# Idle TensorE matmuls rearranged in the opening of a graph-network layer: one, three and nine instead of three, none and three

## The chip, the cores and the metric

One core of a Trainium2 chip runs the whole kernel. The metric is the device time of one execution in microseconds (us). Below, PE is TensorE (its weight loads are PEld), DVE is VectorE, ACT is ScalarE, POOL is GpSimd and SP is the sync engine, which issues the transfers.

## The reference

There are 12500 nodes of width 128 and 200000 edges of width 48, sorted by the node that receives them.

```
h = relu(layernorm(x))
agg = segment_sum(edge_attr, dst, 12500)
z1 = silu(concat(h, agg) @ W1 + b1)        # 176 -> 256
z2 = silu(z1 @ W2 + b2)                    # 256 -> 256
out = x + h + z2 @ W3 + b3                 # 256 -> 128
```

## The kernel before

The nodes are cut into 28 tiles of 448, the edges into groups of 512 (4 edges for each of 128 partitions) and 28 batches of 14 groups and a short last one. A group reaches at most 42 neighbouring nodes, its window. Its segment sum is four small matmuls: the raw edges (128x48) against a one-hot matrix (128x42) that DVE makes by comparing the index rows with a ramp (`make_onehot`, L786). `sum_tile` (L1109, L1112) issues these for a batch: the first seven groups go straight to their place in a bank, the other seven to a staging bank that ACT copies out (`stage_sums`, L554) and POOL adds into `agg_carry` (L498).

The opening prepares the indices, and most of what the change touches lies there. In order of the dependences:

- POOL makes `ident`; PE clears the banks with three matmuls (L1040, L1041) and then runs `WARM0` idle matmuls (L1043). An idle matmul multiplies `ident` by `ident` into a bank nobody reads then. It appears in the trace as two records, as every fp32 matmul does.
- DVE computes the first 128 groups' relative indices (`rel_rows`, L731) and goes on with small index arithmetic until L753. PE turns those rows (`turn_rows(0)`, L1033, four transposes), ACT copies them to `rel` (`rel_of(0)`, L546), and DVE makes the first one-hot matrices (L786).
- ACT makes the other relative rows (L540); `turn_rows(1)`, `turn_rows(2)` and `turn_rows(3)` turn them. The second waits for the offsets that DVE copies (L814), the third follows the loading of offset registers.
- PE then issues `sum_tile(0)`, waits for `s_small` and `s_rel`, counts invalid groups (L1212, L1214), runs `WARM2` idle matmuls (L1217), and issues `sum_tile(1)`, whose last wait is for the one-hot matrices of batch 1. Between them, DVE works a serial list: one-hot matrices of batch 0, the statistics of the first x tile (L761 to L771), two reductions (L725), small steps up to L833, one-hot matrices of batch 1 with `shift_of_norm` (L779) between.
- After `sum_tile(1)` come the turning of the normalized nodes (L1123), the first layer, and the pipeline over the tiles. DVE's `carry_over(0)` (L917) waits for batch 1's sums and for POOL's seven additions of batch 0.

ACT zeroes part of `agg_carry` in two pieces (`clear_carry`, L535): one ahead of `rel_of(0)`, one behind `rel_of(3)` and ahead of the W1 splits (L568, L571). SP issues the transfers of the opening from a fixed list.

Of the kernel before, what the change touches and what calls it, by code (L numbers as in the profile page):

```python
# [33 lines left out]
def gnn_kernel(nc, x, dst, edge_attr, W1, b1, W2, b2, W3, b3, out):  # L34
# [3 lines left out]
    P = 128  # L38
# [10 lines left out]
    TILE = NPG * GPT  # L49
# [11 lines left out]
    ROWS = 4  # L61
# [15 lines left out]
    LOOP, PE_LOOP = (4, 20, 4), (2, 26, 2)  # L77
    LATE_ZEROS = LOOP[0] - 1
    XSLOTS = 4
    WARM0, WARM2 = 3, 3  # L80
    DUMP = 2 * BANK
    NODES = NT * TILE + OVER
    STEPS = NT + 3
# [20 lines left out]
    with ExitStack() as ctx:  # L104
        def sb(name, shape, dt=F32):
            return ctx.enter_context(nc.sbuf_tensor(name, shape, dt))

        def ps(name, shape, dt=F32):
            return ctx.enter_context(nc.psum_tensor(name, shape, dt))

        def sem(name):
            return ctx.enter_context(nc.semaphore(name))
# [14 lines left out]
        ident = sb("ident", [P, P])  # L127
# [26 lines left out]
        agg_carry = sb("agg_carry", [ED, NODES + WINDOW])  # L154

        POOL_ZEROS = 2 * TILE
        ACT_ZEROS = (POOL_ZEROS, 15 * TILE, 20 * TILE)
        POOL_LATE = [(t * TILE, (t + 1) * TILE) for t in range(20, 24)]
        ZEROED = POOL_LATE[-1][1]
        COPIED = NT * TILE - ZEROED  # L160
# [44 lines left out]
        tp = ps("tp", [P, BANK])  # L205
# [35 lines left out]
        s_rel = sem("rel_ready")  # L241
# [63 lines left out]
        def where_invalid(eng, engine_type, body):  # L305

            eng.wait_ge(s_invalid, 1)
            _, (flag,) = nc.values_load_multi_w_load_instructions(
                any_invalid[0:1, 0:1], engines=[engine_type], min_val=0, max_val=NG,
                skip_runtime_bounds_check_because="it counts groups")  # L310
            with eng.If(flag):
                body()
# [140 lines left out]
        def _(pool):  # L453
# [28 lines left out]
            def nodes_of(b):  # L482
                _, nodes = nc.values_load_multi_w_load_instructions(
                    staged_row[0:1, bass.ds(b * SLOT, HALF)], engines=[mybir.EngineType.Pool],
                    min_val=0, max_val=NODES,
                    skip_runtime_bounds_check_because="a valid group's first node is a node, else it is the centre")
                return nodes
# [37 lines left out]
        def _(act):  # L525
# [8 lines left out]
            def clear_carry(a, b):  # L534
                act.activation(agg_carry[:, a:b], zeros[0:ED, :].broadcast_to([ED, b - a]),  # L535
                               ACT.Copy).then_inc(s_carry0_act, 1)
# [6 lines left out]
            def rel_of(c):  # L543
                n = P if c < FULL_ROWS else LAST_G
                act.wait_ge(s_relT, c + 1)
                act.activation(rel[:, c * P:c * P + n, :], rows_turned(c).rearrange("p j r -> p r j"),  # L546
                               ACT.Copy).then_inc(s_rel, 1)
# [9 lines left out]

            clear_carry(*ACT_ZEROS[0:2])
            rel_of(0)
# [3 lines left out]
            for c in range(1, ROWS):  # L563
                rel_of(c)
            clear_carry(*ACT_ZEROS[1:3])
            act.wait_ge(s_w1, W1_LOADS)
# [455 lines left out]
        def _(pe):  # L1022
# [19 lines left out]
            for _ in range(WARM0):  # L1042
# [4 lines left out]
                      start=True, stop=True).then_inc(s_small0T, 1)  # L1047
# [25 lines left out]
            def batch_of(b):  # L1073

                if not isinstance(b, int):
                    return 0, GPT
                return (SHIFT if b == 0 else 0), min(GPT, NG + SHIFT - b * GPT)

            def offsets_of(b):
                first, last = batch_of(b)  # L1080
                _, offsets = nc.values_load_multi_w_load_instructions(
                    direct_row[0:1, bass.ds(b * SLOT, min(last, HALF) - first)], engines=[mybir.EngineType.PE],
                    min_val=0, max_val=DUMP,
                    skip_runtime_bounds_check_because="valid groups lie within SLACK of their tile")
                return offsets
# [3 lines left out]
            def sum_tile(b, parity, offsets):  # L1089

                first, last = batch_of(b)
                wait(pe, s_staged, b)
                wait(pe, s_clear, min(b - 1, NT - 2) if isinstance(b, int) else b - 1)
                for half in range(2):
                    if half * HALF < last:
                        _, _, n, full = groups_of(b, half)
                        slot = 2 * parity + half
                        pe.wait_ge(s_edges[slot], 16 * slot_turn(b, parity) + (16 if full < n else 0))
                        pe.wait_ge(s_onehot, 2 * b + half + 1)
                for at in range(HALF):  # L1100
                    for j in range(PER):
                        for half in range(2):
                            if not first <= at + half * HALF < last:
                                continue
                            rows = P if at < groups_of(b, half)[3] else TAIL_P
                            edges = raw[0:rows, 2 * parity + half, at, j, :]
                            into = onehot[0:rows, 2 * parity + half, at * PER + j, :]
                            if half == 0:
                                mm = pe.matmul(banks[0:ED, bass.ds(offsets[at - first], WINDOW)], edges, into,  # L1109
                                               start=False, stop=True, skip_group_check=True, tile_position=(0, 0))  # L1110
                            else:
                                mm = pe.matmul(stage[ROW2:ROW2 + ED, at * WINDOW:(at + 1) * WINDOW], edges, into,  # L1112
                                               start=(at == 0 and j == 0), stop=True, skip_group_check=True,
                                               tile_position=(0, ROW2))
                mm.then_inc(s_summed, 1)
# [90 lines left out]
            turn_rows(3)  # L1206
            sum_tile(0, 0, offsets)
            offsets = offsets_of(1)
            pe.wait_ge(s_small, 2)
            pe.wait_ge(s_rel, ROWS)  # L1210
            for c in range(FULL_ROWS):
                pe.matmul(invalid_sum[:, 0:1], g["invalid"][:, c:c + 1], one[:, :],  # L1212
                          start=(c == 0), stop=(c == FULL_ROWS - 1))
            pe.matmul(invalid_sum[:, 1:2], g["invalid"][0:LAST_G, FULL_ROWS:ROWS], one[0:LAST_G, :],  # L1214
                      start=True, stop=True, skip_group_check=True).then_inc(s_invalidT, 1)
# [5 lines left out]
            for c in range(1, ROWS):  # L1221
                mm = pe.matmul(nodes_ps[0:PLACE_ROW + 1, c * P:(c + 1) * P], node_place[:, c, :], ident[:, :],
                               start=True, stop=True)
# [25 lines left out]
```

## Time and profile before

| what | value |
|---|---|
| median of 3 runs | 288.13 us |
| the three runs | 288.31, 288.13, 286.89 us |
| profiled execution, its own time | 288.73 us |
| its span | 287.0 us |
| mean granted TensorE clock over the span | 0.994 |

The profile is of one execution. Its span runs from the first to the last instruction, and 1.73 us lie around it. The granted clock is a share of TensorE's full speed: 1.00 is 2.4 GHz, 0.50 is 1.2 GHz. The page shows 1.00 where no change of the clock has been recorded yet, so for the start the durations of the matmuls have to be read as well.

### The profile page before, as it was taken

To read this page: it belongs to the slowest core of one execution; us is meant where nothing else is said; L and a number is where in the kernel's file an instruction comes from. 1 tells how busy PE (TensorE), PEld (TensorE's weight loads), DVE (VectorE), ACT (ScalarE), POOL (GpSimd) and SP (SyncE) were. 2 spreads that over 40 slices of the span, in tenths; PEclk is the share of its full clock that TensorE was granted. 3 is DMA by queue.
4 is the path that set the end of the run, shared out by engine and by line. 5 is a ranking of instruction groups with operands and counts; after the bars stand their busy time and mean duration, and the time that the engine had idled before them with its cause. 6 is when DMAs were issued, how large, how long until landed. Compare 5 with 4: busy or idle time off the path is not lost.

```text
span 287.0 us, 11959 instructions
## 1 busy us (share of the span) xinstructions
PE 274.2 (96%) x4286; PEld 248.4 (87%) x4287; DVE 241.2 (84%) x583; ACT 220.3 (77%) x424; POOL 135.7 (47%) x248
## 2 busy tenths in 40 slices
PE   7868999999999999999999999999999999999994
PEld 3756988999999999999999999999999999999793
DVE  7887998889898898998998889989898888986551
ACT  8856778787886888778877788787976878779662
POOL 4275565454455445454555446454455445452200
PEclk9979999999999999999999999999999999999999
DMA  6998965865688457865687547955687567820112
GB/s 168 323 306 249 204 171 147 248 187 166 170 251 246 142 158 221 256 178 162 182 246 218 173 137 240 256 168 162 187 251 224 149 170 227 253 82 21 30 38 62
DMA packets 79309, 53.28 MB, mean 186 GB/s; under 512 B 2984, under 2 KB 78850, under 8 KB 79288
## 3 DMA queue, kind: packets, MB, share of 16 engines
q1 hardware_dynamic: 79288, 53.04, 63.6%
q8 instruction: 8, 0.13, 0.2%
q14 instruction: 13, 0.11, 0.1%
HBM read 46.29 MB, written 6.40 MB: 184 GB/s over the span
## 4 chain that ended last, share of the span: by engine, by line
PE 85%; DVE 5%; issue 3%; ACT 3%; POOL 2%; ACTq 0%; POOLq 0%; DVEq 0%
PE agg_ps L1109 21%; PE z L1176 15%; PE z L1157 7%; PE z L1161 7%; PE z L1158 7%; PE agg_ps L1112 4%; PE z L1137 4%; PE tp L1123 4%; PE z L1143 4%; PE z L1142 3%; PE z L1139 3%; PE z L1138 3%; DVE onehot L786 2%; PE agg_ps L1040 1%; POOL agg_carry L498 1%
## 5 line engine op out<-in xcount | busy, mean ns | idle before, releaser
L498 POOL TENSOR_TENSOR agg_carry<-staged,agg_carry 48x42 f32 x196 | 92.8, 474 | 77.1 <-ACT staged L554 46.3
L1109 PEld LDWEIGHTS agg_ps<-onehot,raw 128*48 128x48 f32 x1560 | 73.6, 126 | 12.1 <-issue 12.1
L1109 PE MATMUL agg_ps<-onehot,raw 128*48 128x42 f32 x1560 | 77.0, 216 | 3.5 <-DVE onehot L786 3.5
L786 DVE TENSOR_TENSOR onehot<-window,rel 128x1176 f32<-128x1176 f32 (+1 forms) x57 | 77.5, 1363 | 0.5 <-ACT rel L546 0.5
L1112 PE MATMUL agg_ps<-onehot,raw 128*48 128x42 f32 x1568 | 77.2, 216 | 0.0
L1112 PEld LDWEIGHTS agg_ps<-onehot,raw 128*48 128x48 f32 x1568 | 73.9, 127 | 0.0
L479 POOL TENSOR_TENSOR rstd<-vareps,minus_half 128x4 f32<-128x4 f32 (+1 forms) x28 | 37.7, 1346 | 46.4 <-DVE vareps L771 46.4
L1176 PE MATMUL z<-w,h 128*128 128x128 f32 x392 | 51.2, 282 | 1.5 <-ACT h L625 1.1
L625 ACT ACTIVATE h<-z,b2c 128x448 f32<-128x448 f32 (+1 forms) x56 | 35.4, 633 | 19.5 <-PE z L1161 17.1
L1176 PEld LDWEIGHTS z<-w,h 128*128 128x128 f32 x392 | 46.0, 191 | 3.2 <-ACT z L621 1.4
L941 DVE TENSOR_TENSOR h_lo<-h,h_hi 128x448 fp32r<-128x448 f32 (+1 forms) x56 | 34.8, 624 | 12.1 <-ACT h_hi L639 7.6
L635 ACT ACTIVATE h<-z,b1c 128x448 f32<-128x448 f32 (+1 forms) x56 | 35.0, 624 | 11.5 <-PE z L1143 11.5
L1157 PE MATMUL z<-h_hi,w_hi 128*128 128x448 f32 (+1 forms) x112 | 43.1, 385 | 0.0
L593 ACT ACTIVATE xn<-x_t,nmr,rstd 128x128 f32<-128x128 f32 x98 | 40.2, 478 | 1.3 <-DVE nmr L779 1.3
L1158 PE MATMUL z<-h_hi,w_lo 128*128 128x448 f32 (+1 forms) x112 | 40.7, 363 | 0.0
L639 ACT ACTIVATE h_hi<-h 128x448 fp32r<-128x448 f32 (+1 forms) x56 | 32.3, 576 | 1.8
L917 DVE TENSOR_TENSOR agg<-agg_ps,agg_carry 48x448 f32<-48x448 f32 (+1 forms) x28 | 17.2, 614 | 17.5 <-PE agg_ps L1112 17.3
L1161 PE MATMUL z<-h_lo,w_hi 128*128 128x448 f32 (+1 forms) x112 | 31.6, 363 | 0.0
L607 ACT ACTIVATE agg_hilo<-agg 48x448 fp32r<-48x448 f32 (+1 forms) x28 | 16.1, 575 | 11.7 <-DVE agg L917 11.7
L1161 PEld LDWEIGHTS z<-h_lo,w_hi 128*128 128x128 f32 x112 | 21.0, 188 | 1.6
L1158 PEld LDWEIGHTS z<-h_hi,w_lo 128*128 128x128 f32 x112 | 21.1, 189 | 1.2
L1157 PEld LDWEIGHTS z<-h_hi,w_hi 128*128 128x128 f32 x112 | 21.1, 188 | 1.2
(129 smaller groups left out, 411.9 us busy)
## 6 DMA issues: line engine op xcount, KB each, us to landing
raw<-in_edge_attr_dram SPq DMA_DIRECT2D x55, 672.0 KB, 5.9
x_t<-in_x_dram SPq DMA_DIRECT2D x14, 256.0 KB, 6.1
out_dram<-out_t SPq DMA_DIRECT2D x13, 256.0 KB
out_dram<-out_t SPq DMA_DIRECT2D x14, 192.0 KB, 6.0
x_t<-in_x_dram SPq DMA_DIRECT2D x13, 192.0 KB, 6.2
dst_rows<-in_dst_dram SPq DMA_DIRECT2D x1, 512.0 KB
agg_carry<-agg_carry SPq DMA_DIRECT2D x1, 336.0 KB, 8.0
raw<-in_edge_attr_dram SPq DMA_DIRECT2D x1, 288.0 KB, 3.6
```

The source lines that it names most:

```text
L479: pool.tensor_tensor(rstd[:, parity, 0:n], vareps[:, 0:n], minus_half[:, 0:n], ALU.pow).then_inc(s_rstd, 1)
L498: pool.tensor_tensor(into, staged[:, parity, n, :], into, ALU.add).then_inc(s_added, 1)
L593: ln = act.activation(xn[:, parity, q, :], x_t[:, turn, q, :], ACT.Identity, bias=nmr[:, parity, q:q + 1], scale=rstd[:, parity, q:q + 1])
L625: act.activation(h2[:, m, parity * TILE:parity * TILE + n], z[:, m, 0:n], ACT.Silu, bias=b2c[:, m:m + 1]).then_inc(s_h2, 1)
L635: act.activation(h1[:, m, 0:n], z[:, m, 0:n], ACT.Silu, bias=b1c[:, m:m + 1]).then_inc(s_h1, 1)
L786: return dve.tensor_tensor(onehot[:, slot, at * PER:n * PER, :], window[:, :].unsqueeze(1).broadcast_to([P, cols_n, WINDOW]), cols.unsquee ...
L1109: mm = pe.matmul(banks[0:ED, bass.ds(offsets[at - first], WINDOW)], edges, into, start=False, stop=True, skip_group_check=True, tile_posit ...
L1112: mm = pe.matmul(stage[ROW2:ROW2 + ED, at * WINDOW:(at + 1) * WINDOW], edges, into, start=(at == 0 and j == 0), stop=True, skip_group_chec ...
L1157: pe.matmul(z[:, m, 0:n], w2_hi[:, k, cols], h1_hi[:, k, 0:n], start=(k == 0), stop=False)
L1158: pe.matmul(z[:, m, 0:n], w2_lo[:, k, cols], h1_hi[:, k, 0:n], start=False, stop=False)
L1161: mm = pe.matmul(z[:, m, 0:n], w2_hi[:, k, cols], h1_lo[:, k, 0:n], start=False, stop=(k == M - 1))
L1176: mm = pe.matmul(into[0:np_], h2[:, k, a:a + np_], w3[:, k, :], start=False, stop=(k == M - 1), skip_group_check=True)
```

## The change

The idle matmuls in front of the first turns go from three to one (`WARM0`). Three new ones (`WARM1`) are issued behind `sum_tile(0)` and its register loads; the wait for `s_rel` is put in front of them, since they write the bank `tp` that `rel_of(3)` reads. The idle matmuls in front of `sum_tile(1)` go from three to nine (`WARM2`). The border between ACT's two pieces of zeros moves from column 15 x 448 to column 14 x 448, so that 448 columns go from the first piece to the second.

```diff
-    WARM0, WARM2 = 3, 3
+    WARM0, WARM1, WARM2 = 1, 3, 9
...
-        ACT_ZEROS = (POOL_ZEROS, 15 * TILE, 20 * TILE)
+        ACT_ZEROS = (POOL_ZEROS, 14 * TILE, 20 * TILE)
...
             sum_tile(0, 0, offsets)
             offsets = offsets_of(1)
+            pe.wait_ge(s_rel, ROWS)
+            for _ in range(WARM1):
+                pe.matmul(tp[:, 0:P], ident[:, :], ident[:, :], start=True, stop=True)
             pe.wait_ge(s_small, 2)
-            pe.wait_ge(s_rel, ROWS)
             for c in range(FULL_ROWS):
```

## Rows read from the trace of the kernel before

**Rows 1.** The page: busy time of PE, its 40 slices, the granted clock.

```profile
PE 274.2 (96%) x4286; PEld 248.4 (87%) x4287; DVE 241.2 (84%) x583; ACT 220.3 (77%) x424; POOL 135.7 (47%) x248
...
PE   7868999999999999999999999999999999999994
...
PEclk9979999999999999999999999999999999999999
```

**Rows 2.** Windows of 20 us: length, busy of PE, PEld, DVE, ACT, POOL, granted clock, DMA, GB/s.

```profile
0.00:20.00 20.00, 14.02 (x160) 9.90 (x163) 17.52 (x69) 15.67 (x20) 9.32 (x31) 0.95 0.93 261
...
60.00:80.00 20.00, 20.00 (x315) 18.50 (x314) 17.95 (x40) 15.99 (x32) 9.56 (x17) 1.00 0.68 197
```

**Rows 3.** The chain that ended last, in order of time: start, us, what.

```profile
6.11 1.58 PE tp L1043 x6
7.69 0.55 PE z L1033 x4
...
8.27 0.60 ACT rel L546
...
8.90 0.68 DVE onehot L786
...
17.04 1.31 DVE onehot L786
```

**Rows 4.** Windows by stage, columns as in rows 2; the last two of tile agg_ps alone.

```profile
14.50:18.50 4.00, 1.31 (x15) 1.01 (x14) 3.90 (x12) 2.66 (x8) 2.98 (x4) 0.94 1.13 296
18.60:21.30 2.70, 2.70 (x68) 2.70 (x70) 1.63 (x9) 0.70 (x2) 2.00 (x6) 0.50 1.08 317
...
18.50:22.60 4.10, 3.95 (x112) 3.83 (x112) 0.04 (x1) 0.04 (x1) 0.65 1.01 291
28.30:31.10 2.80, 2.72 (x112) 2.61 (x112) 0.00 (x1) 0.00 (x0) 1.00 1.10 183
```

**Rows 5.** Matmuls by line: records, ns min/median/max, first and last start.

```profile
L1043 PE MATMUL tp<-ident x6: 421/421/582, 6.0 to 7.3; 128*128 128x128 f32 x6
...
L1033 PE MATMUL z<-ident,rel_rows x12: 273/285/412, 7.5 to 10.7; 128*128 128x128 f32 x12
...
L1217 PE MATMUL tp<-ident x6: 275/275/377, 16.0 to 16.7; 128*128 128x128 f32 x6
```

**Rows 6.** Timeline of PE: start, us, operation, records, idle before and its releaser.

```profile
11.82 1.50 PE L1112 MATMUL agg_ps<-onehot,raw 128*48 128x42 f32 x29
...
15.66 0.29 PE L1212 MATMUL z<-one,g_invalid 128*1 128x1 f32 x6 [1.12 <-DVE node_place L833]
...
15.99 0.94 PE L1217 MATMUL tp<-ident 128*128 128x128 f32 x6
18.57 0.30 PE L1109 MATMUL agg_ps<-onehot,raw 128*48 128x42 f32 x1 [1.64 <-DVE onehot L786]
```

**Rows 7.** Timeline of DVE in the opening.

```profile
5.83 0.49 DVE L731 TENSOR_SCALAR rel_rows<-dst_rows,g_middle 128x512 f32<-128x512 int32 x1
...
8.18 0.20 DVE L753 TENSOR_SCALAR node_place<-g_moved,g_valid 128x1 f32<-128x1 f32 x1
...
15.44 0.16 DVE L833 TENSOR_SCALAR node_place<-g_chosen 128x3 f32<-128x3 f32 x1
```

**Rows 8.** Timeline of ACT in the opening.

```profile
2.27 5.04 ACT L535 ACTIVATE agg_carry<-zeros 48x5824 f32<-48x5824 f32 x1
...
12.02 2.06 ACT L535 ACTIVATE agg_carry<-zeros 48x2240 f32<-48x2240 f32 x1
14.25 0.42 ACT L568 ACTIVATE w1x_hi<-out_t 128x256 fp32r<-128x256 f32 x1 [0.17 <-DMA out_t<-in_L_gnn_W_dram]
```

**Rows 9.** Timeline of POOL: the last addition of batch 0.

```profile
20.33 0.25 POOL L498 TENSOR_TENSOR agg_carry<-staged,agg_carry 48x42 f32 x1 [0.17 <-POOL agg_carry L498]
```

**Rows 10.** The second load of edges of batch 0: issue, and us to landing.

```profile
L348 SPq DMA_DIRECT2D raw<-in_edge_attr_dram x1: 389/389/389, 5.1 to 5.1; - x1
...
DMA to landing us min/median/max: 5.9/5.9/5.9
```

## The prediction

> **What bounds the kernel now.** I read the page first: PE is busy for 96% of the span, and its slices stand at 9 from the fifth on [rows 1]. The windows sharpen this: PE is busy for all of 20 us in the steady stretch, but for 14.02 us of the first 20 [rows 2]. So the steady part can only be shifted: whatever makes PE start it earlier moves the end by as much, unless another engine or a transfer holds it back. The slices of the granted clock have one dent, in the third [rows 1]. The chain of waits then says what sets the time in the opening, and the windows by stage say at which clock. The reader is to see two places in them.
>
> The first is the way to the first one-hot matrix. It runs through the three idle matmuls, the first turns, ACT's copy and then DVE at 8.90 [rows 3]. The relative rows were there at 5.83 + 0.49 = 6.32 [rows 7], while the turns could be issued only behind the idle matmuls. These ran at half the clock: a record of L1043 took 421 ns, one of the same shape in L1217 took 275 ns [rows 5].
>
> The second is the sum of batch 1. PE waits 1.64 us for DVE's one-hot matrix and starts at 18.57 [rows 6]; the chain comes there from DVE [rows 3]. Before it PE did 1.31 us of work in 4.00 us, and the granted clock fell within that stretch; from 18.60 to 21.30 it stood at 0.50, that is 1.2 GHz, and PE was busy throughout [rows 4].
>
> **The change part by part.** *Two idle matmuls fewer in front of the first turns.* Six records of L1043 take from 6.11 to 7.69, 1.58 us with what overlaps [rows 3]; their starts from 6.0 to 7.3 give about 0.21 us a record once they flow [rows 5]. Four records are thus 0.85 us, and the turns could start 0.85 us earlier, at about 6.63 instead of 7.48, which is still behind the relative rows at 6.32. Four turns were partly at full clock and will now all be at half: 3 x 0.21 + 0.41 = 1.04 us, so they end at 7.67 instead of 8.24: 0.57 us earlier. ACT is free then, as its first clear ended at 2.27 + 5.04 = 7.31 [rows 8] and gets shorter. Its copy of 0.60 us ends at about 8.30. DVE, however, is busy until 8.18 + 0.20 = 8.38 [rows 7], and starts the one-hot matrix at about 8.40 instead of 8.90: a head start of 0.50 us.
>
> Does it reach 18.57? From there DVE works its list with few holes. I looked for waits of its list on others: the x tile, the offsets, POOL's rstd. None of these shows as DVE's releaser except the short one ahead of the first one-hot, so the whole list should move by 0.50. PE's first sums move with it, from 11.82 to 11.32 [rows 6]; the edges they need land at 5.1 + 5.9 = 11.0 [rows 10], which leaves 0.3 us of cover and no more. Beyond that cover the sums would be late, but not DVE's list, which is what counts. Transfers issued behind the sums don't move, because SP is still busy with its fixed list then. I take 0.50 us; the bounds are 0 (something on DVE's list holds it) and 0.57.
>
> *Three idle matmuls behind the first sums.* In the trace PE idles there for 1.12 us until DVE's node_place [rows 6]. Three cost at most 0.94 us, the busy time of the six records of L1217 [rows 6]. The new place of the wait for `s_rel` costs nothing: ACT's last copy ended before its second clear began at 12.02 [rows 8], and the invalid count behind it waits for the same node_place. Cost 0; without the cover, 0.94 us on a count that DVE needs only at the end of its one-hot matrices.
>
> *Nine instead of three in front of the second sums.* With the head start, the count goes from 15.66 to 15.16 and the idle matmuls start at 15.49. Nine cost at most 3 x 0.94 = 2.82 us; without the 0.275 us tail of each set they flow at (0.94 - 0.275)/5 = 0.13 us a record, 18 x 0.13 = 2.4 us. They end between 17.9 and 18.3. The sums can start at 18.57 - 0.50 = 18.07. So they lie in PE's wait, or run over it by at most 0.24 us. I take 0, by the flowing record, since a following matmul doesn't wait for the tail.
>
> *What they do to the clock.* PE's work between 14.5 and 18.5 goes from 1.31 us to roughly 1.3 + 0.8 + 1.6 = 3.7 us of 4. In the trace no stretch so filled lost the clock: it stood at 1.00 wherever PE was busy for nearly all of a window [rows 2, 4]. So I expect the fall to stay away. Its price is read from two batches of the same 112 records: 3.95 us for batch 1, against 2.72 us for batch 2 at full clock [rows 4]. That is 1.23 us. The bounds are 0 (it falls in spite of this) and 1.23.
>
> *Zeros.* A column costs 5.04/5824 = 0.87 ns, so 448 are 0.39 us [rows 8]. The first clear ends at 6.92, in ACT's wait. The second starts 0.5 us earlier, at 11.5, and ends at 11.5 + 2.06 + 0.39 = 13.97, ahead of the W1 transfer that released ACT at 14.25 [rows 8]. Cost 0. If the head start fails, it ends at 14.47 and delays the staged sums by 0.2 us; POOL's additions then end at 20.58 + 0.2, still ahead of the need below.
>
> *Who is late next.* Batch 1's sums end at 18.07 + 2.72 = 20.8 instead of 22.5. DVE's carry_over also needs POOL's last addition of batch 0, 20.33 + 0.25 = 20.58 [rows 9]: 0.2 us of cover, and a bound of 0.2 us on the gain if DVE's work slows POOL more.
>
> **The sum.** -0.50 - 1.23 = -1.73 us, from 288.73 to 287.00 for the profiled execution. That execution was 0.60 us above the median, 288.13, so the median comes to 286.4 us.
>
> **The rivals.**
> *The clock term is missing in the comparison.* One of the three runs took 286.89 us, 1.2 to 1.4 us less than the others, which is the size of the clock's price. Perhaps that execution had no fall. If the typical execution has none, or the fall comes in spite of the idle matmuls, only 0.50 us stay: 287.6 us. For it: the three times spread by just that size. Against it: two of three, and the profiled one, are the long kind. The Trainium skill (TensorE: Matmul & The Clock Gate, Part 1) says that the clock is judged in steps not tied to the start of the kernel, so the same kernel differs from run to run; the one trace here can't show that.
>
> *The head start is lost.* DVE's list is held by a wait that now has slack, or the nine idle matmuls run over: 286.9 us. For it: 0.24 and 0.2 us of cover.
>
> *Everything is given back.* A stretch behind 23 us is set by transfers, and PE waits longer there: 288.1 us. Against it: PE's later waits name DVE and ACT, and DMA was at 0.68 in the steady stretch [rows 2].
>
> *Slower: the clock rises later.* Here it reached full speed during the first turns [rows 5]. With 0.85 us less of idle matmuls ahead, it may stay at half through the first sums. These end at 11.3 + 2 x 2.72 = 16.7. Behind them at half clock come three idle matmuls, 6 x 0.21 = 1.3 us, the count, about 0.6, and nine, 18 x 0.21 = 3.8, so the second sums start at 22.4, and end at 25.1 even at full clock instead of 22.5: +2.6 us, 290.7 us. It decides once the second sums end later than 22.5 + 1.4, so only if half clock lasts through most of the first sums. Against it: the idle matmuls and turns flow almost unbroken from 2 us on, and PE's clock stood at 1.00 over the stretch of turns behind.
>
> A rule speaks for this rival. The turns of 9.5 to 11 us ran at 0.285 us a record, like the fast idle ones [rows 5]; so a stretch made mostly of turns kept the full clock. The Trainium skill (TensorE: Matmul & The Clock Gate, Part 4) says that transposes don't count as PE work for the full clock. By that rule the removed matmuls count and the turns in their place don't, and the time would be this rival's 290.7 us; by the trace, which disagrees as far as keeping the clock goes, it is 286.4 us.
>
> **How the numbers follow.** 0.5% of 288.13 is 1.44 us, about what can be told from no change; faster means below 286.69. Chances: forecast 0.53, clock term missing 0.17, head start lost 0.13, everything given back 0.09, clock rises later 0.08. The forecast's own range is 285.9 to 286.9, and some of it (0.08 of the 0.53) is above 286.69; faster gets 0.45 of it and 0.02 of the lost head start, 0.47. Slower is the last rival, 0.08, and the rest, 0.45, is same. The range leaves out the last rival and the edges: 285.8 to 288.1.
>
> **What would show it.** Right: first turns at about 6.6, first one-hot at 8.4; 24 idle records between the two sums (six and eighteen, where there were six); granted clock 1.00 from 14 to 23; the second sums from 18.1 to 20.8, and the same shift at 28.34 and in the first layer. Wrong: first one-hot still at 8.9; the clock at 0.50 anywhere behind 8 us; PE's wait on DVE gone in front of the second sums because the idle matmuls end later; DVE's carry_over released by POOL; or the shift lost between 23 and 40 us. The forecast fails most easily if other executions have the clock's changes elsewhere than this one.

## The result and the profile after

| | before | after |
|---|---|---|
| median, 12 executions each | 288.22 us | 289.67 us |
| ratio after to before | | 1.0062, interval 1.0040 to 1.0084 |
| profiled execution, its own time | 288.73 us | 290.63 us |
| its span | 287.0 us | 288.9 us |
| its mean granted clock | 0.994 | 0.987 |

The change makes the kernel slower by 0.6%: 1.8 us by the ratio, 1.45 us by the medians. 286.4 us was forecast, in a range of 285.8 to 288.1. The sign is that of the rival to which I gave 0.08. All ratios leave out executions more than 1.5% above the fastest of their kernel; there is one such, in e11 below.

The page of the changed kernel, busy time of PE and granted clock in 40 slices, beside [rows 1]:

```profile
PE 277.3 (96%) x4300; PEld 250.8 (87%) x4301; DVE 241.3 (84%) x583; ACT 220.6 (76%) x424; POOL 133.8 (46%) x248
...
PEclk9779999999999999999999999999999999999999
```

The dent has become two slices wide and starts one slice (7.2 us) earlier. PE's timeline of the changed kernel shows what fell into it; compare [rows 6]:

```profile
6.63 1.06 PE L1033 MATMUL z<-ident,rel_rows 128*128 128x128 f32 x4
...
10.48 1.65 PE L1033 MATMUL z<-ident,rel_rows 128*128 128x128 f32 x8 [1.64 <-ACT rel_rows L540]
...
17.49 1.30 PE L1211 MATMUL tp<-ident 128*128 128x128 f32 x6
18.73 0.29 PE L1214 MATMUL z<-one,g_invalid 128*1 128x1 f32 x6
...
19.06 2.27 PE L1219 MATMUL tp<-ident 128*128 128x128 f32 x18
...
21.27 0.24 PE L1109 MATMUL agg_ps<-onehot,raw 128*48 128x42 f32 x1
```

Its DVE and ACT, beside [rows 3]: the first and the last one-hot matrix ahead of the second sums, then ACT's second set of relative rows and the last of its copies (`rel_of(3)`).

```profile
8.36 0.68 DVE L786 TENSOR_TENSOR onehot<-window,rel 128x504 f32<-128x504 f32 x1
...
16.34 1.38 DVE L786 TENSOR_TENSOR onehot<-window,rel 128x1176 f32<-128x1176 f32 x1
```

```profile
9.71 1.95 ACT L540 ACTIVATE rel_rows<-dst_rows,g_minus_middle 128x512 f32<-128x512 int32 x3 [1.39 <-DMA dst_rows<-in_dst_dram]
...
12.89 0.19 ACT L546 ACTIVATE rel<-tp 128x28 f32<-128x28 f32 x1
```

The windows by stage, beside [rows 4]; columns as there:

```profile
8.85:10.45 1.60, 0.00 (x0) 0.00 (x0) 1.55 (x6) 0.74 (x2) 0.00 (x0) 1.00 1.00 332
10.48:12.10 1.62, 1.62 (x8) 1.13 (x8) 1.59 (x9) 1.62 (x3) 0.07 (x1) 0.81 1.11 344
11.60:18.00 6.40, 6.29 (x89) 5.77 (x88) 5.95 (x17) 5.24 (x10) 2.74 (x5) 0.50 1.04 288
12.90:16.90 4.00, 4.00 (x75) 4.00 (x76) 3.90 (x11) 3.65 (x5) 1.87 (x4) 0.50 1.09 297
21.34:23.99 2.65, 2.65 (x112) 2.53 (x112) 0.00 (x0) 0.00 (x0) 0.83 (x1) 1.00 1.12 328
```

And the chain that ended last, 8 to 24 us, its longest pieces:

```profile
4.81 4.88 DMA dst_rows<-in_dst_dram
10.48 1.65 PE z L1033 x8
12.85 2.48 PE agg_ps L1112 x29
17.49 1.30 PE tp L1211 x6
19.13 2.21 PE tp L1219 x18
```

The reader is to see that the chain no longer comes to the second sums from DVE. It starts at the transfer of the index rows, which landed at 9.71 and released ACT, and then runs through PE alone but for ACT's first piece. DVE was ready at 16.34 + 1.38 = 17.72, 0.6 us earlier than before, as forecast. PE had nothing to do between 8.85 and 10.45. The mean of 0.81 over the 1.62 us that follow means half clock for 0.38 x 1.62 = 0.6 us of them, so the clock fell about 1 us behind the idle stretch, and the first sums ran at 1.2 GHz. They ended at 17.49, against some 14.5 before: 1.0 us of this is the later start behind the index rows, 1.9 us the half clock (4.64 us for the sums instead of 2.7). Only then came the trio, the count and the nine, and the chain goes through both groups of idle matmuls. The second sums started at 21.27, 3.55 us after DVE was ready. They ran at full clock and ended at 23.99, where those of before ended at 22.5. This 1.5 us is close to the difference of the medians. The profiled execution, 1.0 us above its kernel's median, lost about 0.5 us more between 42 and 53 us, which I did not follow: PE's node turns (L1123) of before start at 40.89 and 51.02, those of the changed kernel at 42.36 and 52.97.

### The profile page after: what moved, and what is told of

Same layout as the page of the kernel before. It is cut to its first block, busy times and chain, and to the rows that moved or that the text cites. A ratio compares the mean times of both kernels' runs of the same rounds, so it can differ in the third digit from the quotient of the medians.

```text
span 288.9 us, 11986 instructions
## 1 busy us (share of the span) xinstructions
PE 277.3 (96%) x4300; PEld 250.8 (87%) x4301; DVE 241.3 (84%) x583; ACT 220.6 (76%) x424; POOL 133.8 (46%) x248
## 4 chain that ended last, share of the span: by engine, by line
PE 85%; ACT 3%; issue 3%; DVE 2%; DMA 2%; SPq 1%; POOL 1%; ACTq 0%; POOLq 0%; DVEq 0%
PE agg_ps L1109 21%; PE z L1176 15%; PE z L1157 7%; PE z L1158 7%; PE z L1161 7%; PE agg_ps L1112 5%; PE z L1137 4%; PE tp L1123 4%; PE z L1143 3%; PE z L1142 3%; PE z L1139 3%; PE z L1138 3%; DMA dst_rows<-in_dst_dram 2%; POOL agg_carry L498 1%; DVE onehot L786 1%
## 5 line engine op out<-in xcount | busy, mean ns | idle before, releaser
L498 POOL TENSOR_TENSOR agg_carry<-staged,agg_carry 48x42 f32 x196 | 91.0, 464 | 81.3 <-ACT staged L554 52.6
L635 ACT ACTIVATE h<-z,b1c 128x448 f32<-128x448 f32 (+1 forms) x56 | 35.0, 624 | 11.5 <-PE z L1143 11.5
```

The lines of the kernel that those rows point to most:

```text
L498: pool.tensor_tensor(into, staged[:, parity, n, :], into, ALU.add).then_inc(s_added, 1)
L635: act.activation(h1[:, m, 0:n], z[:, m, 0:n], ACT.Silu, bias=b1c[:, m:m + 1]).then_inc(s_h1, 1)
```

## The experiments

All times are medians of 10 to 12 executions; the ratio is to the kernel before on the same chip, and is not the quotient of the two medians beside it, from which it differs by up to 0.3%. The three numbers name the idle matmuls at the front, behind the first sums, and ahead of the second sums; "gap" are those that I put between L1046 and the second turns. The kernel before is 3, 0, 3 and the changed one 1, 3, 9.

| run | idle matmuls | us | before, us | ratio, interval |
|---|---|---|---|---|
| e1 | 1, 0, 3 | 287.04 | 287.35 | 0.9981, 0.9965 to 0.9998 |
| e2 | 3, 3, 9 | 289.96 | 287.35 | 1.0063, 1.0036 to 1.0089 |
| e3 | 1, 3, 3 | 288.29 | 287.35 | 1.0025, 1.0009 to 1.0042 |
| e4 | 3, 0, 3, zeros moved | 287.50 | 287.35 | 0.9997, 0.9973 to 1.0020 |
| e5 | 3, 0, 9 | 288.67 | 287.58 | 1.0016, 0.9995 to 1.0037 |
| e6 | 1, gap 4, 3, 9 | 287.87 | 287.58 | 1.0003, 0.9986 to 1.0021 |
| e7 | 1, gap 4, 0, 3 | 287.55 | 287.58 | 1.0002, 0.9981 to 1.0022 |
| e8 | 1, 0, 0 | 287.00 | 287.58 | 0.9970, 0.9952 to 0.9988 |
| e9 | 1, gap 4, 0, 8 | 287.59 | 287.55 | 0.9993, 0.9971 to 1.0014 |
| e10 | 1, 0, 9 | 288.82 | 287.55 | 1.0047, 1.0028 to 1.0067 |
| e11 | 0, 0, 0 | 286.80 | 287.55 | 0.9971, 0.9949 to 0.9992 |
| e12 | 3, gap 4, 0, 3 | 287.68 | 287.55 | 1.0002, 0.9977 to 1.0026 |

Zeros are moved in e2, e3 and e6 too, as in the changed kernel. The results also give the mean granted clock of every execution, and it falls into steps: 1.00, 0.994, 0.988, 0.982. 0.988 means twice as much time at half clock behind the first recorded change as 0.994. In each of the six profiles that read 0.987 or 0.988 (after, e1, e2, e4, e8, e10) this is one unbroken stretch, twice as long as that of [rows 4]: from 11.5 to 18.3 us in the changed kernel, from 8.7 to 15.5 us in e1. In the profiles at 0.994 it is a short one, and it can lie early (e3, 11.3 to 14.6 us) or late (before, e7 and e12, from about 18 us). So the mean clock says how long the clock was down, not where. The count in each step, with the median of those executions:

| kernel | 1.00 | 0.994 | 0.988 | 0.982 |
|---|---|---|---|---|
| before, with e1 to e4 | 9: 287.21 | 16: 287.46 | 8: 287.81 | |
| before, with e5 to e8 | 7: 287.15 | 16: 287.51 | 12: 287.81 | |
| before, with e9 to e12 | 7: 286.84 | 13: 287.55 | 15: 287.63 | |
| after | | | 10: 289.60 | 2: 290.88 |
| e1 (1, 0, 3) | | | 12: 287.03 | |
| e2 (3, 3, 9) | 2: 287.37 | 1: 289.92 | 7: 290.05 | |
| e3 (1, 3, 3) | | 1: 287.50 | 9: 288.18 | 2: 289.05 |
| e4 (3, 0, 3, zeros moved) | 3: 287.08 | 6: 287.94 | 3: 287.57 | |
| e5 (3, 0, 9) | 2: 286.91 | 3: 288.08 | 7: 288.84 | |
| e6 (1, gap 4, 3, 9) | 9: 287.73 | 3: 288.52 | | |
| e7 (1, gap 4, 0, 3) | 4: 287.44 | 8: 288.03 | | |
| e8 (1, 0, 0) | | | 11: 286.99 | 1: 287.00 |
| e9 (1, gap 4, 0, 8) | 6: 287.56 | 6: 287.65 | | |
| e10 (1, 0, 9) | | 1: 288.05 | 9: 288.75 | 2: 289.38 |
| e11 (0, 0, 0) | 2: 287.84 | | 8: 286.55 | 2: 289.06 |
| e12 (3, gap 4, 0, 3) | 7: 287.18 | 4: 288.72 | 1: 289.56 | |

**Which part costs.** The first four runs each take one part alone or back.

```diff
-    WARM0, WARM2 = 3, 3
+    WARM0, WARM2 = 1, 3
```

> The kernel before with one idle matmul instead of three in front of the first turns; nothing else is changed. Theory 1: the fewer idle matmuls at the front decide about the clock, since PE then works less ahead of the first sums; the granted clock falls near 12 us and the first sums run at half clock, as in the profile of the changed kernel, where they ended at 17.49 instead of 14.54. The span's mean clock is then near 0.988 or below. Behind them come only three idle matmuls and no trio, so the second sums start near 19 us and the time is 287.5 to 288.5 us, less than the changed kernel's 289.7. Rival (the queue): the idle matmuls in front of the sums cost the time and the front does nothing; clock 0.994 as before, time 287.7 to 288.2 us.

The mean clock did as theory 1 said, 0.988 in all twelve. The time was 287.04 us, a little under before and below the forecast 287.5. So half clock in the first sums costs almost nothing by itself. In its profile the clock fell earlier than theory 1 had it, at about 8.7 us, and was back at 15.5. The window from 9 to 15 us, and PE ahead of the second sums:

```profile
9.00:15.00 6.00, 5.17 (x51) 4.82 (x53) 5.82 (x23) 5.69 (x9) 2.74 (x5) 0.50 1.10 320
```

```profile
16.99 0.29 PE L1212 MATMUL z<-one,g_invalid 128*1 128x1 f32 x6 [0.58 <-issue]
...
17.33 0.94 PE L1217 MATMUL tp<-ident 128*128 128x128 f32 x6
...
18.19 0.24 PE L1109 MATMUL agg_ps<-onehot,raw 128*48 128x42 f32 x1
```

The second sums start at 18.19, earlier than the 18.57 of [rows 6], although most of the first ran at half clock: PE's waits of 1.12 and 1.64 us had held room for that.

```diff
-    WARM0, WARM1, WARM2 = 1, 3, 9
+    WARM0, WARM1, WARM2 = 3, 3, 9
```

> The changed kernel with three idle matmuls at the front again: three, three and nine, zeros as changed. Theory 1: with the front back the clock stays up from the first turns through the second sums; mean clock 0.999 or so, second sums from about 18.6 to 21.3 us, 286.9 to 287.1 us. Rival (the queue): twelve idle matmuls between the sums push the second sums back; the time stays near 289.7 us.

Theory 1 falls here. Three at the front again, and the time stays at 289.96 us. The two executions in which the clock stayed up took 287.37, the seven at 0.988 took 290.05.

```diff
-    WARM0, WARM1, WARM2 = 1, 3, 9
+    WARM0, WARM1, WARM2 = 1, 3, 3
```

> The changed kernel with three instead of nine idle matmuls in front of the second sums: one, three and three. Its twelve records fewer at the 0.12 us that they took in the profile of the changed kernel (2.21 us for eighteen) are 1.5 us. Theory 1 with the queue as its price: the first sums still run at half clock, and the second sums start 1.5 us earlier, 288.2 us, if the clock has risen by then. If it has not, the second sums run at half clock and the time is 289.5 us or more. If the idle matmuls were all hidden, it stays at 289.7 us.

288.29 us, 1.4 us below the changed kernel's median (1.1 us by the ratios, 1.0025 against 1.0062): the six idle matmuls lay on the path. Against e1 the trio costs 1.25 us, together with the moved zeros, which the next run has alone.

```diff
-        ACT_ZEROS = (POOL_ZEROS, 15 * TILE, 20 * TILE)
+        ACT_ZEROS = (POOL_ZEROS, 14 * TILE, 20 * TILE)
```

> The kernel before with only the border of ScalarE's two pieces of zeros moved by 448 columns. Theory 1: no difference within 0.2 us, clock 0.994 as before. Rival (zeros): the longer second piece delays the weight splits and the staged sums, and the time rises by 0.2 to 0.4 us.

No difference that can be told: the interval, 0.9973 to 1.0020, is 0.8 us below to 0.6 us above, so the rival's 0.2 to 0.4 us is not excluded. Its profile also fell into an execution in which the kernel otherwise like before has the early fall:

```profile
12.90:16.90 4.00, 3.89 (x73) 3.76 (x72) 3.90 (x10) 3.02 (x5) 2.58 (x5) 0.50 1.10 291
```

```profile
16.91 0.29 PE L1212 MATMUL z<-one,g_invalid 128*1 128x1 f32 x6
...
17.24 1.46 PE L1217 MATMUL tp<-ident 128*128 128x128 f32 x6
18.67 0.23 PE L1109 MATMUL agg_ps<-onehot,raw 128*48 128x42 f32 x1
```

So the first sums at half clock are no product of the change alone. The profile I predicted from showed one kind of execution of before; this is another, in which PE comes to the count at 16.91 instead of 15.66 and there is no wait left for more idle matmuls to hide in.

**The queue theory and the gap theory.** My new theory had two parts. In executions whose first sums run at half clock, PE is late, and each idle matmul behind them delays the second sums (the queue). And the early fall comes from PE's idle stretch between L1046 and the second turns (the gap).

```diff
-    WARM0, WARM2 = 3, 3
+    WARM0, WARM2 = 3, 9
```

> The kernel before with nine instead of three idle matmuls in front of the second sums; front three, no trio. Queue theory: PE is late in the executions whose first sums run at half clock, so the six extra ones delay the second sums by 12 records x 0.12 = 1.4 us there, and lie in PE's wait for DVE in the executions at full clock. A third to two thirds of the executions of before are of the late kind, so the median is 287.6 to 288.8 us, with a spread between executions at 1.00 (near 287.2 us, as before) and the others. Clock theory (the one the prediction rested on): the nine keep the clock up for the second sums, 286.9 us or less.

As the queue theory says: 286.91 us in the two executions at full clock, 288.84 in the seven at 0.988, and 288.08 in the three between. The interval of the ratio still takes in 1, with executions that differ so.

```diff
+    MID = 4
...
                       start=True, stop=True).then_inc(s_small0T, 1)
+            for _ in range(MID):
+                pe.matmul(tp[:, 0:P], ident[:, :], ident[:, :], start=True, stop=True)
```

> The changed kernel with four more idle matmuls, placed in PE's wait between the turning of the first offsets and the second turns, where it idled 1.64 us in the changed kernel's profile; the other numbers stay one, three and nine. Gap theory: that idle stretch is what makes the clock fall near 12 us; filled, the clock stays at 1.00, the first sums end by 15 us, all twelve idle matmuls behind them are hidden again, and the time is 286.7 to 287.3 us, 2.5 us less than the changed kernel. Rival (the front decides, or the clock falls whatever is in the gap): the fall stays, mean clock 0.988, and the time is 289.7 us or up to 0.5 more.

This is the changed kernel with four idle matmuls more, and it is 1.8 us faster by the medians (ratio to before 1.0003 against 1.0062). Not one of its executions is at 0.988. PE in its profile, where the line numbers are three higher behind the new lines, and the window of the first sums:

```profile
8.77 1.16 PE L1050 MATMUL tp<-ident 128*128 128x128 f32 x8
9.88 1.30 PE L1034 MATMUL z<-ident,rel_rows 128*128 128x128 f32 x7
...
15.34 0.91 PE L1214 MATMUL tp<-ident 128*128 128x128 f32 x6 [0.46 <-issue]
...
16.51 2.28 PE L1222 MATMUL tp<-ident 128*128 128x128 f32 x18
...
18.71 0.24 PE L1112 MATMUL agg_ps<-onehot,raw 128*48 128x42 f32 x1
```

```profile
12.90:16.90 4.00, 3.54 (x86) 3.27 (x84) 3.90 (x11) 3.77 (x7) 2.15 (x4) 1.00 1.14 294
```

The time is 0.6 us above the 287.3 of the expectation. The nine end near 18.7, and the second sums start there, 1.1 us behind DVE, whose last one-hot matrix is ready at 17.65 in this profile. So even at full clock the twelve were not wholly hidden.

> One idle matmul at the front, four in the gap ahead of the second turns, none behind the first sums and three ahead of the second. Gap theory: mean clock 0.994 to 1.000; the 0.5 us of head start stays; 286.4 to 286.9 us, against 287.0 for the same kernel without the four. Rival (half clock in the first sums is hidden in PE's later waits anyway): no difference from 287.0 us. Rival (front decides): clock 0.988 and 287.0 us or more.

287.55 us: no gain over e1, as the second theory's rival had it. None of its executions is at 0.988, eight are at 0.994. The profiled one, 288.95 us, has the late fall of [rows 4]: the second sums start at 18.06, with 1.23 us of wait for DVE ahead, and run at half clock from about 18.3 to 21.7. The eight are not all alike: four took 287.3 to 287.6 us, as those at 1.00 did, and four 288.5 to 288.95, so only the latter look like the profiled one.

> One idle matmul at the front and none between the sums. Queue theory: where the first sums run at half clock, the three in front of the second sums are on PE's path too; without them the second sums start up to 0.9 us earlier, as soon as DVE's one-hot matrix is there (18.0 us): 286.2 to 286.7 us, against 287.0 with the three. Rival (the three hold the clock up for the second sums): these run at half clock more often, and the time is 287.5 to 288.3 us.

287.00 us, ratio 0.9970. None of the three is needed to bring the second sums to full clock in its profile:

```profile
16.85 0.29 PE L1212 MATMUL z<-one,g_invalid 128*1 128x1 f32 x6 [0.50 <-issue]
...
17.90 0.23 PE L1109 MATMUL agg_ps<-onehot,raw 128*48 128x42 f32 x1 [0.64 <-DVE onehot L786]
```

```profile
12.10:16.10 4.00, 4.00 (x79) 4.00 (x79) 3.90 (x10) 3.20 (x6) 2.61 (x5) 0.54 1.13 302
18.00:20.60 2.60, 2.60 (x112) 2.50 (x112) 1.58 (x9) 1.00 (x3) 1.76 (x7) 1.00 0.97 270
```

The first sums, stretched by the half clock, fill most of the time up to DVE, and the clock came back while they ran, at about 15.8 us, with no idle matmul ahead but the one at the front. The gain over e1 was to be 0.3 to 0.8 us: by the ratios it is 0.3 us, at the lower end and within both intervals.

**Doses and the ends.** Four more, cut from the same lines.

> One idle matmul at the front, four in the gap ahead of the second turns, none behind the first sums, eight ahead of the second. In the profile with three there, PE waited 1.23 us behind them, room for five more at 0.24 us each. Gap and queue theories together: the first sums and the second run at full clock in nearly all executions (mean clock 1.00), nothing runs over, 286.5 to 287.0 us. Rival (half clock in the first sums is hidden anyway, and DVE's list sets the start of the second): no better than one at the front and none between the sums, 287.0 us. If they run over DVE: 287.3 us or more.

The clock is better kept (six at 1.00, six at 0.994) and the second sums start at 18.06 and run at full clock in the profile, yet 287.59 us is no better than before. It did not do what I expected.

> One idle matmul at the front, no trio, nine ahead of the second sums: the changed kernel without the trio, with the old zeros. Queue theory: between one-and-three (287.0 us) and the changed kernel (289.7 us); six more than the first are 12 records x 0.12 = 1.5 us, of which up to 0.2 us may be hidden, so 288.3 to 288.6 us, and all executions alike, mean clock 0.988. Rival (the trio alone makes the loss): 287.0 to 287.3 us.

288.82 us; 1.8 us over e1 by the medians, 1.9 us by the ratios (0.0066 x 287.5). The six extra are on the path. With intervals of some 0.5 us either way on each ratio, this is no clear difference from the 1.5 us of their records.

> The kernel before with no idle matmul at all. If idle matmuls are worth something here, the second sums or the stretch behind run at half clock, and the time is 288.3 us or more (1.2 us for the second sums). If the first sums at half clock bring the clock up by themselves and the wait for DVE hides them, it is 286.7 to 287.3 us, like one at the front and none between the sums.

286.80 us, ratio 0.9971. None of the sets of idle matmuls tried here does better than none. Two things in its executions: the profiled one shows what the mean clock hides, as the page gives 1.00 where no rise has been recorded:

```profile
12.10:16.10 4.00, 4.00 (x78) 4.00 (x76) 3.86 (x12) 3.13 (x5) 2.71 (x5) 1.00 1.13 303
```

```profile
11.84 2.55 PE L1112 MATMUL agg_ps<-onehot,raw 128*48 128x42 f32 x29
...
18.00 0.30 PE L1109 MATMUL agg_ps<-onehot,raw 128*48 128x42 f32 x1 [0.93 <-DVE onehot L786]
```

29 records in 2.55 us instead of the 1.50 of [rows 6]: this was half clock, and a record of 0.30 us at 18.00, where e8 has 0.23, says that it still was when the second sums started. That execution took 287.86 us. And one of the twelve took 291.35 us.

> The kernel before with four more idle matmuls in the gap ahead of the second turns; three, none and three otherwise. Gap theory: the early fall near 12 us disappears, so mean clocks are 1.00 or 0.994 and none 0.988; where a fall remains it is the late one, ahead of the second sums, as in the first profile, and costs 1.2 us there: two kinds of executions, near 287.2 and near 288.5 us. Rival (the gap has nothing to do with it): the same mixture of clocks as the kernel before.

One of twelve at 0.988, where the gap theory had none, against 35 of the 103 executions of before; the rest in two kinds, 287.18 and 288.72 us, as the gap theory has it. The 1.5 us between them is near the 1.23 us that I took for second sums at half clock.

## Why the prediction was wrong, point by point

**The head start was right.** DVE's first one-hot matrix came at 8.36 (8.40 forecast, 8.90 before) and the last was ready at 17.72, 0.6 us earlier. e1, which has this part alone, is 0.3 us faster by the medians and 0.5 us by the ratio, which has an interval of 0.06 to 1.0 us.

**The zeros and the new place of the wait**: no cost shows. e4 has none beyond its interval. The wait was not tried alone, but in the changed kernel's profile ACT's last copy ended at 12.89 + 0.19 = 13.08, long before PE came to the wait at 17.49.

**The step that failed is the cover of the idle matmuls**, in the words of the prediction: "So they lie in PE's wait, or run over it by at most 0.24 us. I take 0", and for the trio "Cost 0; without the cover, 0.94 us". The waits of 1.12 and 1.64 us behind the first sums were read from one execution in which these ran at full clock. In the changed kernel's profile they took 4.64 us (12.85 to 17.49) instead of 2.7, and had started 1.0 us later, behind index rows that landed later. The late landing is not the change's doing: with the same front and zeros, e3's profile has its first sums at 11.52. The second sums waited for PE. In terms of that profile: PE came out of the first sums 2.95 us late; the trio, the count and the nine took 3.78 us; so the start went from 18.57 to 21.27, +2.70; full clock gave 1.22 back; +1.48 at the end of the second sums. The runs price the same terms: trio 1.25 us (e3 against e1), six more 1.4 us (after against e3; 1.1 by the ratios) or 1.8 (e10 against e1), and nearly all of it returns when the gap is filled and the first sums run at full clock (e6). The terms do not add up exactly: with nine behind it the trio costs 0.4 us by the ratios, 0.85 by the medians (after against e10), where it costs 1.25 with three. The spread of the executions is too wide to say whether that is real.

**The clock's term was mis-sized.** I priced one stretch at half clock by the second sums alone, 1.23 us, and took the profiled execution, and with it two of the three at hand, for the typical kind. Of the 103 executions of before, 23 are at 1.00 and show no stretch to regain behind the first recorded change. The 45 at 0.994 fall apart: 34 took 286.8 to 287.83 us, and 11 took 288.3 to 289.0. The profile that I predicted from, 288.73 us with the late fall, is of the kind of the 11. By the medians, 0.994 goes with 0.25 to 0.7 us more than 1.00, and 0.988 with 0.6 to 0.8 us. So for the median kernel there was well under 1.23 us to regain. A stretch in the first sums is mostly hidden in the waits (e1); a late one costs, as in e12. Which kind an execution is can be seen in its profile, not in its mean clock.

The rule that I drew for the clock was also against my own rows: it did not stand at 1.00 wherever PE was busy. From 18.60 to 21.30 PE was busy throughout at 0.50 [rows 4], and so it was from 12.90 to 16.90 in the changed kernel. The rows showed that the clock had not fallen in a filled stretch; they did not show that filling one brings it back at once.

**The rivals.** "The clock rises later" had the right sign and the right place, half clock in the first sums with the idle matmuls queued behind; its 290.7 us stands near the 290.63 of the profiled execution, which is luck in part: that execution is 1 us above the median, its first sums took 4.64 us and not 2 x 2.72 = 5.44, and the nine ran at full clock. Its cause was wrong in two ways. The clock did rise, and fell again at about 11.5 us. And the two matmuls removed from the front were not what made the loss: with them back it stays (e2). They do go with the clock: with three at the front 68 of the 103 executions of before are at 0.994 or 1.00, with one at the front and the gap open it is two of the 60 in after, e1, e3, e8 and e10. But in e1 that costs nothing. The rule of the Trainium skill (TensorE: Matmul & The Clock Gate, Part 4) that transposes don't count as PE work for the full clock, which I had set against the trace, isn't decided by this: the fall came behind a stretch with no PE work at all, and turns followed.

The other rule, in the Trainium skill's same page, Part 1, is that the clock is judged in steps not tied to the kernel's start, so that a kernel differs from run to run. The difference from run to run is borne out: before shows mean clocks of 1.00, 0.994 and 0.988 in 23, 45 and 35 of 103 executions. The reason given for it is not tested by any run here.

**What stays open.** How the gap acts. Of the 60 executions with one at the front and the gap open (after, e1, e3, e8, e10), 58 are at 0.988 or below, and of the 36 with four in the gap (e6, e7, e9) none is; that much is shown. That the idle stretch in the gap is what makes the clock fall is not shown, and the kept profiles speak against it as the whole cause. In those of e1, e8 and e10 the clock fell at 8.7 to 8.9 us, before or at the start of the gap, behind an earlier idle stretch of 1.31 us ahead of L1046, which the four matmuls don't fill. For e8:

```profile
8.80:9.20 0.40, 0.04 (x1) 0.00 (x0) 0.37 (x3) 0.40 (x1) 0.00 (x0) 0.65 1.11 332
```

And in e3's profile the clock fell at 11.3 us although the gap was only 0.39 us wide, while before kept its clock with 0.69 us:

```profile
9.53 1.47 PE L1033 MATMUL z<-ident,rel_rows 128*128 128x128 f32 x8 [0.69 <-ACT rel_rows L540]
```

```profile
9.22 1.42 PE L1033 MATMUL z<-ident,rel_rows 128*128 128x128 f32 x8 [0.39 <-ACT rel_rows L540]
...
11.60:14.40 2.80, 2.80 (x44) 2.80 (x45) 2.66 (x11) 2.77 (x4) 2.37 (x5) 0.50 1.11 309
```

The first line is from PE's timeline of before, the other two from e3's timeline and windows. Four matmuls in the gap may as well shorten a stretch at half clock as prevent one; the mean clock would show less time down either way. Further: why e9, with the clock mostly up and the idle matmuls hidden in its profile, is no faster than before. Why e2 and e5 are at 0.988 in seven executions of ten and of twelve, more often than before is, when their first matmuls are the same up to the first sums. And the 0.5 us that the changed kernel's profile loses between 42 and 53 us.

**The better version.** One at the front and none between the sums, or none at all: 0.3% under before (0.9970 and 0.9971), 0.9% under the changed kernel by the ratios. The second sums are then released by DVE's list, at 17.90 in e8's profile and 18.00 in e11's.

## What to carry to other kernels

A wait seen in one profile is no room to put work in until it is known how long the work in front of it takes when the clock is down: idle matmuls stand in the same queue as the real ones, and they are dear just in the executions in which they were meant to help. Look at the granted clock of many executions, not of one, before pricing such a stretch. And where a wait follows, work at half clock may be free, because it fills the wait: in e1 and e8 it did, and the clock was back before the second sums.

## What the runs showed of the hardware

- With identical programs the fall of the clock came early, late or not at all from one execution to the next, and the index rows landed at different times: ACT was released by them at 9.71 in the changed kernel's profile, while before it had them by 8.76, when its first copy allowed it to start.
- Behind 1.60 us without PE work the clock fell (after, at 11.5 us); with eight idle records in that place it stayed at 1.00 through the first sums (e6). The length of that stretch doesn't decide by itself: 0.39 us, and a fall, in e3's profile; 0.69 us, and none, in that of before.
- Half clock for all of the 112 records of a batch's sums makes them 4.64 us (after, first sums) against 2.72 us at full clock (after, second sums), 1.7 times as long and not twice.
- PE busy for 4.00 us out of 4.00 with the small sums at half clock did not bring the clock up within that stretch (after, 12.90 to 16.90), while in e8 it rose within one just like it (0.54 over 12.10 to 16.10).
